# Moving the last two gates from GpSimd to VectorE, and weaving the input products between the scans

## The reference

```
xs, z = split(x @ in_w)                      # 512 channels each
xc    = silu(conv4(xs) + cb)
dt, B, C = split(xc @ xp_w)                  # 16 states
delta = softplus(dt @ dt_w + dt_b)
h     = h * exp(delta * A) + (delta * xc) * B    # step by step along the sequence
y     = sum over states of h * C  +  xc * D_skip
x     = layer_norm((y * silu(z)) @ out_w + x) * w + b
```

## Time and profile before

| | |
|---|---|
| median of three runs | 8184.75 us (8182.96 to 8188.17) |
| the profiled execution, its own time | 8188.17 us |
| its span, first to last instruction | 8186.4 us |
| busy over the span: VectorE, GpSimd | 95%, 87% |
| busy over the span: TensorE, ScalarE | 80%, 68% |
| mean granted TensorE clock | 0.896 of full speed |

### The profile page before, as it was taken

The page is one execution under the profiler, slowest core; times in us unless marked ns, Lnnn a source line. Parts: engine busy times, 40 slices in busy tenths (PEclk is TensorE's granted clock), DMA queues, the critical chain, the costliest instruction groups (busy, mean ns, idle before and its releaser), DMA issues. The chain is left out here.

```text
span 8186.4 us, 75757 instructions
## 1 busy us (share of the span) xinstructions
PE 6535.1 (80%) x21028; PEld 2516.5 (31%) x21028; DVE 7762.7 (95%) x7283; ACT 5596.6 (68%) x9717; POOL 7135.4 (87%) x3572
## 2 busy tenths in 40 slices
PE   5878788787777888888888888878777888775888
PEld 2223232232222333233222323223222332222555
DVE  8999999999999999999999999999999999996776
ACT  5677777777767777677777777777776777763444
POOL 3899999999999999999999999999999999995555
PEclk8898888999899889898888988999899888987999
DMA  6554455544544455554555445454455545551110
GB/s 183 118 121 109 107 127 116 119 120 111 133 116 116 102 118 123 121 122 105 128 117 122 109 109 124 116 131 109 113 129 116 116 103 117 123 120 52 38 38 25
DMA packets 566030, 909.27 MB, mean 111 GB/s; under 512 B 58368, under 2 KB 200192, under 8 KB 564352
## 3 DMA queue, kind: packets, MB, share of 16 engines
q1 hardware_dynamic: 565632, 904.73, 46.6%
HBM read 715.55 MB, written 188.94 MB: 110 GB/s over the span
## 5 line engine op out<-in xcount | busy, mean ns | idle before, releaser
L921 POOL TENSOR_TENSOR hc<-h,crep 128x1024 f32<-128x1024 f32 x2048 | 4775.9, 2364 | 486.0 <-PE acc L474 337.4
L1060 DVE TENSOR_TENSOR_SCAN h<-dA,carry,bu 128x512 f32<-128x512 f32 x3072 | 3686.6, 1260 | 22.1 <-ACT dA L630 21.0
L630 ACT ACTIVATE dA<-drep,cur 128x512 f32<-128x512 f32 x4096 | 2619.2, 712 | 150.0 <-DMA drep<-delta_dram 113.9
L1045 DVE TENSOR_TENSOR bu<-durep,B_all 128x1024 f32<-128x1024 f32 x2048 | 2393.6, 1214 | 112.3 <-DMA durep<-du_dram 63.3
L456 PE MATMUL B_all<-dtc,spread_b 128*128 128x512 f32 x2048 | 1291.2, 716 | 1262.2 <-DVE bu L1045 1261.0
L474 PE MATMUL acc<-hc,gather 128*32 128x512 f32 x8192 | 1324.7, 716 | 9.0 <-POOL hc L921 9.0
L1060 DVE TENSOR_TENSOR_SCAN h<-dA,bu 128x512 f32<-128x512 f32 x1024 | 1167.6, 1200 | 39.5 <-POOL hc L921 39.3
L639 ACT COPY carry<-h 128x4 f32<-128x4 f32 x1023 | 198.5, 194 | 1343.3 <-DVE h L1060 1341.6
L498 PE MATMUL work<-xT,inw 128*128 128x512 f32 x2048 | 1006.5, 636 | 13.7 <-ACT sz L733 9.1
L508 PE MATMUL work<-xs,taps 128*128 128x512 f32 x2048 | 959.0, 611 | 0.0
L456 PEld LDWEIGHTS B_all<-dtc,spread_b 128*128 128x128 f32 x2048 | 371.7, 209 | 1896.8 <-DVE bu L1045 1809.2
(11 more groups left out here) (181 smaller groups left out, 7000.8 us busy)
## 6 DMA issues: line engine op xcount, KB each, us to landing
drep<-delta_dram SPq DMA_DIRECT2D x1024, 256.0 KB, 6.6
durep<-du_dram SPq DMA_DIRECT2D x1024, 256.0 KB, 7.4
crep<-c_dram SPq DMA_DIRECT2D x1024, 64.0 KB, 6.7
delta_dram<-za SPq DMA_DIRECT2D x64, 1024.0 KB, 4.2
du_dram<-relu SPq DMA_DIRECT2D x64, 1024.0 KB, 5.3
x_res<-xbuf SPq DMA_DIRECT2D x64, 512.0 KB, 3.8
xbuf<-x_res SPq DMA_DIRECT2D x64, 512.0 KB, 6.3
xc<-xbuf SPq DMA_DIRECT2D x63, 512.0 KB, 4.3
```

The costliest lines, as they stand in the source:

```text
L630: act.activation(dA[:, 4 * (s % 2) + k, :], drep[q % 2][:, k, :], ACT.Exp, scale=cur[:, p_, 4 * s + k:4 * s + k + 1]).then_inc(da_ready, 1)
L921: pool.tensor_tensor(hc[:, pair, :], h[:, pair, :], crep[:, j:j + 1, :].to_broadcast([P, 2, T]), ALU.mult).then_inc(hc_ready, 1)
L1045: dve.tensor_tensor(bu[:, 2 * k:2 * k + 2, :], durep[q % 2][:, 2 * k:2 * k + 2, :], B_all[:].unsqueeze(1).to_broadcast([P, 2, T]), ALU.mul ...
L1060: dve.tensor_tensor_scan(h[:, r, :], dA[:, r, :], bu[:, k, :], start, ALU.mult, ALU.add).then_inc(scanned, 1)
```

## The change

Three things are edited.

1. The gates of blocks 1 and 3 go to VectorE as one instruction each, like the other two: in turn 10, and in turn 2 of the next chunk, behind the first scan. ScalarE's copies (`take_sums`) and GpSimd's multiplications are gone, and so is the semaphore `gated` with its waits.
2. On VectorE the two `times_b` of a group no longer stand in a row behind the four scans of the group before. The one with k = 0 stands before the last scan of the previous turn, the one with k = 1 behind the first scan of its own turn.
3. On ScalarE `copy_xT` in turn 11 moves from ahead of the exponentials to behind them, and `root_guess` moves from turn 12 to turn 11, ahead of `copy_xT`.

```
@@ ScalarE @@
-            def take_sums(n, q):
-                act.wait_ge(summed, 2 * (NG * n + QS * (q + 1)))
...
-                act.copy(sums[:, 0, :], acc[:]).then_inc(acc_read, 1)
             def squares(m):
                 act.wait_ge(mean_ready, m + 1)
-                act.wait_ge(gated, 2 * m + 2)
@@ ScalarE, turn @@
                     keep_states(group(g, s - 1))
-                    if s == 2 and not is_first(g):
-                        take_sums(g - 1, DB - 1)
-                    if s == 10:
-                        take_sums(g, 1)
-                    if s == 11 and not is_last(g) and not (isinstance(g, int) and g == TOT - 2):
-                        copy_xT(g + 2)
                     exp(group(g, s + 1), here if s + 1 < NG else other)
...
-                        if s == 12:
+                        if s == 11:
                             root_guess(g - 1)
                     if not is_last(g):
                         if not (isinstance(g, int) and g == TOT - 2):
+                            if s == 11:
+                                copy_xT(g + 2)
@@ GpSimd, turn @@
-                    if s == 2 and not is_first(g):
-                        gate(g - 1, other, DB - 1)
-                    if s == 10:
-                        gate(g, 1 - other, 1)
@@ VectorE, turn @@
                     scan(at, ph, 0)
-                    if s in (6, 14):
+                    if s == 2 and not is_first(g):
+                        gate(g - 1, other, DB - 1)
+                    if s in (6, 10, 14):
                         gate(g, here, (s - 6) // 4)
-                    for k in range(1, 4):
-                        scan(at, ph, k)
-                    for k in range(2):
-                        times_b(nxt, k)
+                    times_b(at, 1)
+                    scan(at, ph, 1)
+                    scan(at, ph, 2)
+                    times_b(nxt, 0)
+                    scan(at, ph, 3)
```

More of the change, by code:

```diff
@@ L158, in mamba_layers @@
             sem(n) for n in ("da_ready", "bb_ready", "bu_ready", "scanned", "hc_ready", "summed", "carried"))
-        acc_read, gated, row_summed, mean_ready, squared, var_ready, lnv_done, guess_ready, newton, root_done, normed, weighted, x_ready = (
-            sem(n) for n in ("acc_read", "gated", "row_summed", "mean_ready", "squared", "var_ready", "lnv_done", "guess_ready", "newton",
+        acc_read, row_summed, mean_ready, squared, var_ready, lnv_done, guess_ready, newton, root_done, normed, weighted, x_ready = (
+            sem(n) for n in ("acc_read", "row_summed", "mean_ready", "squared", "var_ready", "lnv_done", "guess_ready", "newton",
                              "root_done", "normed", "weighted", "x_ready"))
@@ L527, in project_out @@
                 if j == 0:
-                    pe.wait_ge(gated, 2 * (m + 1))
                     pe.wait_ge(acc_read, DB * (m + 1))
@@ L899, in _ @@
             turns(act, turn)
-            take_sums(TOT - 1, DB - 1)
             for j in range(2):
@@ L922, in times_c @@
                                        ALU.mult).then_inc(hc_ready, 1)
[L924 to L928, removed]
             def silu_xc(n, p_):
@@ L1023, in _ @@
             turns(pool, turn)
-            gate(TOT - 1, 1, DB - 1)
             mean(TOT - 1)
@@ L1164, in _ @@
             dve.wait_ge(piece_copied, PIECES)
-            times_b(group(0, 0), 1)
             def turn(g, ph):
@@ L1171, in turn @@
                     scan(at, ph, 0)
-                    if s in (6, 14):
+                    if s == 2 and not is_first(g):
+                        gate(g - 1, other, DB - 1)
+                    if s in (6, 10, 14):
                         gate(g, here, (s - 6) // 4)
-                    for k in range(1, 4):
-                        scan(at, ph, k)
-                    for k in range(2):
-                        times_b(nxt, k)
+                    times_b(at, 1)
[3 more added lines that the diff above has]
+                    scan(at, ph, 3)
             turns(dve, turn)
+            m = TOT - 1
+            gate(m, 1, DB - 1)
 class Fp4:
```

## The result

The changed kernel takes 8295.15 us (8294.17 to 8296.07) against 8184.72 us (8182.96 to 8188.17): ratio 1.0135, 95% interval 1.0122 to 1.0148. The profiled execution's span is 8296.2 us, 109.8 more than before.

What follows compares the result with a forecast made beforehand. GpSimd and ScalarE, in a closed loop with VectorE, were taken to set the pace by about 1 us. Loop +1.7 and TensorE +1.2 gave +2.9 per chunk, +180 us: 8365 us (forecast 8295 to 8415, range 8225 to 8440).

Steps and rivals of the forecast that it cites:

- it waits as now, +105: Bound of the uncertain term: VectorE's turn 3 wait for TensorE stays as before; +1.7 us per chunk, +105 us.
- a chain that had led by 1 us: Closed loop through VectorE, ScalarE, GpSimd and the load, 113.71 us per chunk, leading VectorE's own work by about 1 us.
- Gates on the chain: Turn 10's gate leaves GpSimd's stretch, -1.26 us; turn 2's enters VectorE's, +0.58 us, per chunk.
- part c: Loop stretch on GpSimd from softplus down to relu: 43.27 us before, 42.0 forecast.
- part a: VectorE's loop stretch, new chunk's first product through turn 4's last scan to ScalarE's start: 34.9 us without idle, 37.9 forecast.
- The weave on part a: Last scan of turn 4 moves from 2.25 us before the turn's end to its end; +3.0 us, the gate's 0.58 included.
- b: Loop stretch on ScalarE down to quad, until GpSimd starts softplus: 20.01 us, forecast to stay.
- TensorE in turn 2: Broadcast starts 2.90 us later, saves a 1.14 pause; VectorE's turn 3 wait goes from 0.8 to 2.0, +1.2 per chunk.
- TensorE is in time: Rival, chance 0.22: at the faster clock TensorE's broadcast is in time; +58 to +105 us, 8240 to 8290 us.
- copy_xT: In turn 11 ScalarE waits 2.8 us for variance, TensorE up to 2; 1.3 are free there, so nothing is counted.
- the prediction's own list: Signs of being wrong: period under 114 us, no durep wait at the chunk's end, or VectorE waits for dA in turn 8.
- Relief: Rival, chance 0.1: 1.26 us off GpSimd brings durep in time and VectorE never waits; -68 us, 8117 us.

Runs made afterwards that it cites:

- The experiment for the last scan's place: Changed kernel with copy_xT and root_guess in their old places and the product k = 0 behind the last scan: 8284.27 us (ratio 1.0121).
- the weave with the early copy: Kernel before with only the woven product order, and ScalarE's copy of acc (block 3) moved from turn 2 into turn 1: 8348.35 us (ratio 1.0201).
- The lengthened GpSimd: Changed kernel with one more 128 x 512 product on GpSimd in turn 10, on a scratch tile: 8362.47 us (ratio 1.0217).

## Why the prediction was right, and where it was too high

The direction and the mechanism were right, and the range held. The single forecast, 8365 us, was 70 too high, and that the 8295.15 measured falls at the very edge of the forecast's 8295 to 8415 is luck: the case that came true is the one that the sum names as "it waits as now, +105", 8290 us. Slower was forecast because the weave moves the last scan of turn 4 to the turn's end, and a chain that had led by 1 us grows by it. Step by step:

- *Gates on the chain.* Forecast: -1.26 in part c, +0.58 in part a. Part c is 42.0, and the kernels with one gate moved gave 8110 and 8184 us. Shown, once the shorter wait in turn 3 is counted with the second.
- *The weave on part a.* Forecast 37.9 and TensorE's wait: 38.7 with a wait of 0.85. Forecast for b: 20.0, measured 20.0. Over chunks 4 to 61 the parts average 35.5, 20.0, 43.3 and 15.6 before and 38.3, 20.0, 42.0 and 15.8 after. The experiment for the last scan's place brought a cost of its own, but the weave with the early copy against the kernel before shows that place at some 2.3 per chunk, where the forecast had 2.4, with TensorE's wait nearly the same. The lengthened GpSimd shows that the chain leads, or very nearly.
- *TensorE in turn 2.* This is the term that was mis-sized. "It starts 2.90 later and saves the 1.14" gave 1.3 in the fast case, 2.25 in the slow, 2.0 on average. Measured 0.85 in this chunk, and 0.70 on average over chunks 4 to 61, where it was 0.79 before: the stretch to the next broadcast is 9.65, not the 10.4 to 11.3 that the rows gave less the pause. I had taken the pause for its own length, and the clock as given. The pause also held the clock down, and in the woven order the kernels with it and without it differ by twice its length. So the term was 1.2 us per chunk too much, 74 us, and that is all of the 70 by which the sum is too high. The rival "TensorE is in time" was half right: its ground (the faster clock, and less work behind a wait for ScalarE) was the right one, but TensorE stayed as late as before, and the measured time is 5 us above its 8290.
- *copy_xT.* Forecast: ScalarE stands 2.8, TensorE up to 2, nothing in the sum. Measured 2.39 and 1.25; VectorE waits for it by the most of all its waits, and undoing it changes the time by nothing. The wait used up what the chain had left free, and therefore those for `durep`, which I expected at 1 us per chunk, were nearly unseen. By the prediction's own list two signs of being wrong are there in part, almost no wait for `durep` and 4.7 us of waits for `dA` in turn 8; neither overturns the chain, since undoing this edit brings `durep` back to 51.8 us at the same time.
- *Relief.* The rival was true of the gates, -59 us, and not of the whole. Its condition, a chain shorter than VectorE's own path, holds as soon as the weave is undone: all waits of the gates alone come to 41 us.

What stays open: how the weave's 172 us behind the gates divide between the last scan's place and TensorE's later start. By the timelines the wait in turn 3 is 0.15 us with the gates alone and 0.85 in the changed kernel with edit 3 undone, so an estimate for TensorE's part is 0.7 of the 2.7 to 2.8 us per chunk. No kernel with the gates isolates it.

## What to carry over

When several engines form a closed loop that is about as long as the busiest engine's own work, price an edit on the loop first: moving the gate of turn 10 took 1.26 us from GpSimd and was worth 1.2 per chunk, although it added 0.58 to the 95% busy VectorE beside the loop. The largest wait of a profile need not be a cost: ask what it would be replaced by. And in weaving, look at which instruction of a group others wait for, and keep that one early.

## What the runs showed of the hardware

- A scan that needs the product directly ahead of it started 1.29 us after it, against 1.13 where that product is not the one it needs: 0.16 us per such pair, 16 pairs per chunk (the kernel with the product k = 0 behind the last scan).
- A pause of 1.2 us (average) in TensorE's work, right after an idle time of 4.8, cost 2.3 us per chunk in the woven order: the granted clock over the stretch was 0.66 with it and 0.79 without it. In the old order, where `project_x` then waited 1.5 us for `xc`, taking the pause out gave 15 us in all, 0.2 per chunk.
